# A decoder layer with routed experts: the low parts of w1 and w3 made once per expert and loaded from DRAM, in place of a subtraction per block

## The reference, cut to what matters

```python
x = layernorm(x + attn(x))                 # 8192 tokens of 128
x = layernorm(x + cross(x, ctx))
flat = x.reshape(-1, 128)
probs = softmax(flat @ gate_W.T); top_v, top_i = top_k(probs, 2)          # 8 experts, 2 per token
g = silu(einsum('td,edf->etf', flat, w1_e)); u = einsum('td,edf->etf', flat, w3_e)    # f = 512
routed = gates @ einsum('etf,efd->etd', g * u, w2_e)
shared = mean over 8 shared experts of (silu(x @ w1_s) * (x @ w3_s)) @ w2_s
out = layernorm(x + 0.5 * shared + 0.5 * routed)
```

## Time and profile before

| | |
|---|---|
| time, median of 3 runs | 739.44 us (737.78 to 742.28) |
| the profiled execution | 737.8 us |
| its span | 736.0 us |
| PE busy | 663.8 us, 90% |
| DVE, ACT, POOL busy | 511.9, 469.2 and 468.0 us |
| mean granted clock of TensorE | 0.964 of full |
| DMA | 72.70 MB, mean 99 GB/s |
| chain that ended last | PE 70%, DVE 13%, POOL 5%, ACT 5% of the span |

### The profile page before, as it was taken

One profiled execution on the slowest core, in us unless ns is written; L12 is line 12 of the kernel. 1 busy time (PEld: TensorE's weight loads), 2 busy tenths in 40 slices (PEclk: granted clock), 3 DMA queues, 4 the chain that ended last, 5 costly groups with the idle time before them and its releaser, 6 DMA issues.

```text
span 736.0 us, 16511 instructions
## 1 busy us (share of the span) xinstructions
PE 663.8 (90%) x5112; PEld 621.0 (84%) x5113; DVE 511.9 (70%) x1426; ACT 469.2 (64%) x1434; POOL 468.0 (64%) x471
## 2 busy tenths in 40 slices
PE   4899999978799999999999999999999999999700
PEld 3688888877588887899999999999999999998600
DVE  2689999986999973466556555565556555647995
ACT  4899999963389852365565455455555555646885
POOL 3488888886010147748888777777777777771332
PEclk9899999999989999999999999999999999999955
DMA  8467555553211216211111111121111212227683
GB/s 231 129 203 235 180 181 171 183 174 115 72 31 56 59 51 176 79 30 41 44 41 44 49 51 51 47 54 50 50 54 50 51 48 52 50 78 202 167 234 86
DMA packets 87250, 72.70 MB, mean 99 GB/s; under 512 B 10066, under 2 KB 72410, under 8 KB 87194
## 3 DMA queue, kind: packets, MB, share of 16 engines
q1 hardware_dynamic: 77808, 53.43, 24.7%
q0 software_dynamic: 9088, 18.63, 9.4%
q10 hardware_dynamic: 298, 0.01, 0.0%
HBM read 50.14 MB, written 21.89 MB: 98 GB/s over the span
## 4 chain that ended last, share of the span: by engine, by line
PE 70%; DVE 13%; POOL 5%; ACT 5%; issue 5%; DMA 1%; SPq 0%; POOLq 0%; DVEq 0%; ACTq 0%
PE bank L1516 16%; PE bank L1481 9%; PE bank L1483 9%; PE bank L1482 9%; PE bank L1142 5%; PE bank L547 4%; PE bank L1131 3%; PE bank L1132 3%; PE bank L1133 3%; POOL y_rows L1425 3%; PE bank L542 2%; DVE xg L1820 2%; PE bank L1473 2%; ACT ev L708 2%; PE bank L572 2%
## 5 line engine op out<-in xcount | busy, mean ns | idle before, releaser
L1611 DVE TENSOR_TENSOR s_hT<-s_sg,bank 128x512 f32<-128x512 f32 x142 | 97.7, 688 | 140.3 <-ACT s_sg L1552 80.9
L1425 POOL DMA_INDIRECT y_rows<-e_y,dst_tab x142 | 152.4, 1073 | 50.2 <-issue 42.0
L1417 POOL DMA_INDIRECT xg<-x_rows,src_tab x142 | 145.8, 1027 | 46.3 <-issue 39.6
L1481 PE MATMUL bank<-e_x_hi,e_w_hi 128*128 128x256 f32 x568 | 172.1, 303 | 0.0
L1483 PE MATMUL bank<-e_x_hi,e_w_lo 128*128 128x256 f32 x568 | 160.6, 283 | 0.0
L1482 PE MATMUL bank<-e_x_lo,e_w_hi 128*128 128x256 f32 x568 | 160.5, 283 | 0.0
L1516 PE MATMUL bank<-w,s_hT 128*128 x1136 | 138.2, 275 | 0.0
L1516 PEld LDWEIGHTS bank<-w,s_hT 128*128 128x128 f32 x1136 | 133.0, 192 | 0.0
L1558 ACT ACTIVATE e_y<-bank 128x256 f32<-128x256 f32 x71 | 27.2, 384 | 147.1 <-DMA y_rows<-e_y,dst_tab 111.7
L1482 PEld LDWEIGHTS bank<-e_x_lo,e_w_hi 128*128 128x128 f32 x568 | 109.1, 192 | 0.0
L1481 PEld LDWEIGHTS bank<-e_x_hi,e_w_hi 128*128 128x128 f32 x568 | 108.6, 191 | 0.0
(11 more groups left out here) (170 smaller groups left out, 1453.8 us busy)
## 6 DMA issues: line engine op xcount, KB each, us to landing
yk<-y_rows SPq DMA_DIRECT2D x16, 512.0 KB, 4.3
xT_in<-in_xT_dram SPq DMA_DIRECT2D x16, 256.0 KB, 3.0
x_res<-in_x_dram SPq DMA_DIRECT2D x16, 256.0 KB, 3.2
w_all<-in_L_ffn_w_e_dram SPq DMA_DIRECT2D x16, 256.0 KB, 4.0
c_in<-in_ctx_dram SPq DMA_DIRECT2D x16, 256.0 KB, 2.9
cT_in<-in_ctxT_dram SPq DMA_DIRECT2D x16, 256.0 KB, 3.1
x_rows<-x SPq DMA_DIRECT2D x16, 256.0 KB, 2.4
x2T_cols<-x2T SPq DMA_DIRECT2D x16, 256.0 KB, 2.8
```

The source lines that it names most:

```text
L1417: nc.gpsimd.indirect_dma_start(xg[b % XR][:, t, :], None, x2_rows, bass.IndirectOffsetOnAxis(src_tab[:, i:i + 1], 0)).then_inc(gathered[b ...
L1425: nc.gpsimd.indirect_dma_start(y_rows, bass.IndirectOffsetOnAxis(dst_tab[:, n:n + 1], 0), y[b % R][:, t, :], None).then_inc(scattered[b % ...
L1481: nc.tensor.matmul(at, w_hi[r % WR][:, w], x_hi[r % R][:, :], start=True, stop=False)
L1611: nc.vector.tensor_tensor(hT[par][:, half * HC:(half + 1) * HC, :].rearrange("p c n -> p (c n)"), sg[half][:, :], bank[2 + half][:, :], AL ...
```

## The change

The low part of w1 and w3 depends only on the expert. The change makes it once for each of the 8 experts, in the routing stage, and keeps the 8 in a DRAM tensor `w_lo_rows`, 512 KB each. ScalarE makes a high part into one of two tiles `split_hi`, GpSimd subtracts into one of two tiles `split_lo`, SP stores. In the experts stage SP loads the low part of each block by one DMA of 512 KB, and VectorE's `w_low` is gone. ScalarE still makes the high part for each block.

```diff
@@ attention, scalar, last
             if i == NG + 3:
                 take_x2T(*at(5))
+                act.wait_ge(all_ld, 16 * 3 * E)
+                split(0)
+                split(1)
                 early(0)
...
@@ routing, sync
+        def store_low(e):
+            sp.wait_ge(split_lo_ok, e + 1)
+            sp.dma_start(w_lo_rows[ds(e * P, P), :], split_lo[e % 2][:, :].bitcast(F32)).then_inc(split_stored[e % 2], 16)
         def rest():
             sp.wait_ge(attended.l_ps, NG)
             for g in range(EARLY):
                 if g + 3 < EARLY:
                     load_x(g + 3)
                 sp.dma_start(x2_all[:, ds(g * GT, GT), :], group_rows(x2_rows, g)).then_inc(all_ld[g // 2], 16)
+                if g < 2:
+                    for e in range(4 * g, 4 * g + 4):
+                        store_low(e)
@@ routing, gpsimd
+        def split(e):
+            pool.wait_ge(split_hi_ok, e + 1)
+            if e >= 2:
+                pool.wait_ge(split_stored[e % 2], 16 * (e // 2))
+            nc.gpsimd.tensor_tensor(split_lo[e % 2][:, :], columns_of(e), split_hi[e % 2][:, :].bitcast(F32),
+                                    ALU.subtract).then_inc(split_lo_ok, 1)
         def rest():
+            pool.wait_ge(attended.all_ld, 16 * 3 * E)
+            for e in range(4):
+                split(e)
             x_low(2)
+            for e in range(4, E):
+                split(e)
             x_low(3)
@@ routing, scalar
+        def split(e):
+            if e >= 2:
+                act.wait_ge(split_lo_ok, e - 1)
+            nc.scalar.activation(split_hi[e % 2][:, :], columns_of(e), ACT.Copy).then_inc(split_hi_ok, 1)
         def rest():
             for n in range(PRE, EARLY * FC):
                 chunk(n)
+                if 2 <= n - PRE + 2 < E:
+                    split(n - PRE + 2)
                 if 0 <= n - C0 < NC:
                     codes(n - C0)
@@ experts
+    def sync(sp):
+        at_reg = sp.alloc_register("e_lo_at")
+        sp.wait_ge(late.w_at_ok, 1)
+        for n in range(2):
+            sp.wait_ge(late.split_stored[n], 16 * (E // 2))
+        for b in range(NB):
+            sp.reg_load(at_reg, w_at[0:1, ds(b, 1)])
+            at = sp.snap(at_reg, min_val=0, max_val=(E - 1) * P)
+            if b >= WR:
+                sp.wait_ge(u_ps, (b - WR + 1) * 2)
+            sp.dma_start(w_lo[b % WR][:, :].bitcast(F32), w_lo_rows[ds(at, P), :]).then_inc(w_lo_ld[b % WR], 16)
...
-                pe.wait_ge(w_lo_ok, b + 1)
+                pe.wait_ge(w_lo_ld[r % WR], 16 * (j * (TURN // WR) + r // WR + 1))
...
-        def w_low(b):
-            dve.reg_load(at_reg, w_at[0:1, ds(b, 1)])
-            at = dve.snap(at_reg, min_val=0, max_val=(E - 1) * P)
-            if b >= WR:
-                dve.wait_ge(u_ps, (b - WR + 1) * 2)
-            dve.wait_ge(w_hi_ok, b + 1)
-            nc.vector.tensor_tensor(w_lo[b % WR][:, :], columns(w_all, at), w_hi[b % WR][:, :].bitcast(F32),
-                                    ALU.subtract).then_inc(w_lo_ok, 1)
```

More of the change, by code:

```diff
@@ L104, in __init__ @@
         self.w_at_ok = sem("w_at_ok")
+        self.split_hi = [one(f"split_hi{n}", [P, 2 * F], F32R) for n in range(2)]
+        self.split_lo = [one(f"split_lo{n}", [P, 2 * F], F32R) for n in range(2)]
+        self.split_hi_ok, self.split_lo_ok = sem("split_hi_ok"), sem("split_lo_ok")
+        self.split_stored = [sem(f"split_stored{n}") for n in range(2)]
 @dataclass
@@ L217, in _ @@
                     rest()
-                    two.sync(sp)
+                    late_x, out_rows_of = two.sync(sp)
+                    late_x()
+                    one.sync(sp)
+                    out_rows_of()
                 @block.gpsimd
@@ L239, in _ @@
                     ahead, run = one.scalar(act)
-                    early, rest = zero.scalar(act, ahead)
-                    first.scalar(act, early)
+                    early, split, rest = zero.scalar(act, ahead)
+                    first.scalar(act, early, split)
                     rest()
@@ L689, in tensor, with scalar @@
         pe.wait_ge(w2s_ld, 16)
-    def scalar(act, early):
+    def scalar(act, early, split):
         act.dma_start(bq_two[:, :].rearrange("a (j d) -> a j d", j=GT),
@@ L1219, in rest @@
                 ahead(n - EARLY * FC)
-        return chunk, rest
+        return chunk, split, rest
     def vector(dve, ahead):
@@ L1394, in experts @@
     w_hi = ring("w_hi", [P, 2 * F], F32R, n=WR)
+    y = ring("y", [P, BT, D])
     w_lo = ring("w_lo", [P, 2 * F], F32R, n=WR)
-    y = ring("y", [P, BT, D])
     sg, hT = late.sg, late.hT_of_block
-    w_hi_ok, w_lo_ok, xT_ps, x_hi_ok, x_lo_ok, g_ps, u_ps, sg_ok, h_ok, y_ps, y_ok = (
-        sem(f"e_{n}") for n in "w_hi_ok w_lo_ok xT_ps x_hi_ok x_lo_ok g_ps u_ps sg_ok h_ok y_ps y_ok".split())
+    w_hi_ok, xT_ps, x_hi_ok, x_lo_ok, g_ps, u_ps, sg_ok, h_ok, y_ps, y_ok = (
+        sem(f"e_{n}") for n in "w_hi_ok xT_ps x_hi_ok x_lo_ok g_ps u_ps sg_ok h_ok y_ps y_ok".split())
+    w_lo_ld = [sem(f"e_w_lo_ld{n}") for n in range(WR)]
     LATE_AT = (NB - 2, NB - 1)
@@ L1699, in store, with late_x, rest @@
             sp.dma_start(group_rows(out_rows, g), res[g % 2][:, :, :]).then_inc(stored[g % 2], 16)
-        LAG = R + 2
-        for i in range(4):
-            load_x(i)
-        for n in range(RING):
-            sp.wait_ge(scattered[n], 16 * BT * len(range(n, NB, RING)))
-        nx = 4
-        for g in range(NG + LAG):
-            if g < NG:
-                load(g)
-            while nx < LATE and FC * (nx - 1) + 1 < LEAD + 2 * (g - R + 2):
-                load_x(nx)
-                nx += 1
-            if g >= LAG:
-                store(g - LAG)
-        for n in range(2):
-            sp.wait_ge(stored[n], 16 * (NG // 2))
+        def late_x():
+            for i in range(2):
+                load_x(i)
+        def rest():
+            LAG = R + 2
+            for i in range(2, 4):
+                load_x(i)
+            for n in range(RING):
+                sp.wait_ge(scattered[n], 16 * BT * len(range(n, NB, RING)))
+            nx = 4
+            for g in range(NG + LAG):
+                if g < NG:
+                    load(g)
+                while nx < LATE and FC * (nx - 1) + 1 < LEAD + 2 * (g - R + 2):
+                    load_x(nx)
+                    nx += 1
+                if g >= LAG:
+                    store(g - LAG)
+            for n in range(2):
+                sp.wait_ge(stored[n], 16 * (NG // 2))
+        return late_x, rest
     def tensor(pe):
```

17 lines of the change are left out of this document (8 added, 9 removed).

## The result

| | before | after |
|---|---|---|
| time, median | 739.4 us (737.78 to 742.28) | 748.5 us (746.89 to 749.12) |
| ratio | | 1.0119, 95% interval 1.0098 to 1.0141 |
| the profiled execution | 737.8 us | 746.89 us |
| its span | 736.0 us | 745.2 us |
| DVE, ACT, POOL busy | 511.9, 469.2, 468.0 us | 438.7, 486.6, 468.5 us |

The change makes the kernel slower by 9.1 us, 1.2%. VectorE lost 73 us of work, and hardly any of that shows in the time.

A forecast was written before the change was run, and what follows sets the result against it. TensorE bounds the experts, and VectorE's chain to the first one-hots delays routing's table. Routing's +9.0 us less 0.7 us for shorter transfers gives +8.3 us: 739.4 + 8.3 = 747.7 us, range 740.5 to 753 (8 in 10).

The forecast's parts named there:

- What bounds the kernel: Experts: TensorE busy for all 346.04 us, 4.87 us a block; routing's table: three engines close to full, started by VectorE's chain.
- What is removed: Experts: 71 VectorE subtractions, 87.1 us, give nothing themselves; GpSimd's indirect transfers shorten, so the last scatter starts 0.7 us earlier.
- The experts' loads: Experts: 71 loads of 512 KB on SP, landing in 4.3 us with 14.6 us of lead, cost nothing.
- rival of late loads: Experts: low-part loads arrive late and TensorE waits at each block; 18 us more, 766 us; chance 0.07.
- first step: Routing, ScalarE: two high parts ahead of the last `x2T` delay it by 1.2 us; picks move from 184.9 to 186.0 us.
- Second step: Routing, GpSimd and stores: split 2 waits for store 0 until 191.5 us, then a nearly closed row of splits follows.
- Third step: Routing: VectorE's chain to the first one-hots waits for GpSimd's splits, 8.2 us in the first walk.
- collisions in the table's first rounds: Routing's table: further collisions of splits with one-hots were put at nothing, as TensorE is then the slower one.
- the signs: Expected in traces: TensorE's pre-table wait 10 us or more, first experts block at 319 to 321, `pos` operations 1.5 to 3 us.
- the splits hide: Routing rival: GpSimd's operations mostly miss VectorE's exposed ones; +1 to +4 us, 740.5 to 743.5 us; chance 0.24.
- ScalarE does wait for the splits: Routing rival: ScalarE's high parts wait for GpSimd and hold up the silus; +13 to +16 us, 752 to 756; chance 0.09.
- Nothing was faster: Experts rival: relieving GpSimd's backlog drops the pace below 4.87 us a block; 733 to 738 us with hidden splits; chance 0.04.

The follow-up runs named there:

- the experts' part alone: Against the changed kernel: no splits or stores in routing; each block's 512 KB load reads another tensor, same traffic, low parts wrong; 738.73 us, ratio 0.9993.
- the kernel with loads behind block b-2: Against the changed kernel: each low-part load in the experts is issued when block b-2's up products are done, not b-4's; 747.65 us, ratio 1.0109.
- the kernel with the small subtraction: Against the changed kernel: GpSimd's subtraction in routing covers 8 of 1024 columns; high parts, stores and waits stay; 742.09 us, ratio 1.0045.

## Why the prediction was right

**What bounds the kernel.** Right as put. The experts' stretch is 346.04 us in both kernels, and what VectorE loses there is not time. The kernel with the experts' part alone shows it by itself: within 1 us of before.

**What is removed.** The mechanism is as told: the transfers fell from 2.02 to 0.97 us, and the mean of 142 scatters to 975 ns, against 1063 where the subtraction stands in the experts. The size, 0.7 us, was too large for what reaches the end. The last scatter:

```profile
669.56 0.96 POOL L1482 DMA_INDIRECT y_rows<-e_y,dst_tab  x1 [0.30 <-issue]
```

It follows the experts' first matmul by 349.02 us; before it was 349.52. That is 0.5 us, of which 0.43 arrive at VectorE's first weighting of the combine stage. And most of that did not last: at VectorE's products in the combine stage there is a pause of 0.29 us that before has not, marked as issue, with no releaser in the trace. Behind it the lag behind before is 9.12 us, where it had been 8.77. Why it pauses there stays open; a third of a microsecond was not worth a run.

**The experts' loads: nothing.** Right. The landing time was taken as 4.3 us and is 3.7 where it can be read, in the kernel with loads behind block b-2. The lead was taken as 14.6 us and is 16.0. The DMA share rose from 0.18 to 0.50 of 4.87 us a block, so by an estimate from these a load takes 1.6 us of the DMA engines' time, not the 2.4 of my expectation above. The rival of late loads is out.

**Routing, first step.** Right to a tenth: the picks start at 186.55 us in place of 184.87, 1.68 us later, 0.59 of which are the drift of that execution. The rest, 1.09, was put at 1.2 (1.1 for the picks). The rows of ScalarE, beside the earlier trace rows:

```profile
176.60 0.60 ACT L772 ACTIVATE x2T<-bank 128x512 f32<-128x512 f32 x1 [1.91 <-PE bank L550]
177.09 2.00 ACT L1250 ACTIVATE split_hi<-w_all 128x1024 fp32r<-128x1024 f32 x2
...
183.21 0.60 ACT L772 ACTIVATE x2T<-bank 128x512 f32<-128x512 f32 x1 [0.56 <-PE bank L550]
```

**Second step.** The order of GpSimd's work was forecast as it fell: split 2 at 191.5 (191.83), `x_lo` at 196.5 (196.51), split 4 at 198.5 (198.21). From there the splits stood closer than I had them: split 6 ended at 205.73 and not at 207, since neither ScalarE's high parts nor the stores made GpSimd wait between them, as I had it in my walk.

**Third step.** The term was mis-sized in both of its parts, and the two errors nearly cancel. I had four waits, of 1.6, 2.4, 1.8 and 2.4 us, 8.2 together. There are four, and they measure 1.73 - 0.69 = 1.04, 2.66 - 0.69 = 1.97, 1.53 - 0.23 = 1.30 and 2.35 - 0.23 = 2.12 us (the short values from the kernel with the small subtraction, where the conversion and the shift each take 0.23 us): 6.4 us. The one-hots come clear of split 6. The first are done at 207.39 + 1.04 = 208.43 us, and not at 209.7.

Against that stands the sentence that collisions in the table's first rounds cost nothing, "as TensorE is then the slower one". That was wrong. Split 7 and the two operations behind it stretched a one-hot to 3.21 us and another to 1.88 us, and VectorE lost the little lead it had. Before, its row shows four waits in these rounds, of 0.68, 0.19, 0.19 and 0.22 us, three for TensorE and one for ScalarE, 1.28 together, and none behind the last of them until 259.60:

```profile
217.91 0.69 DVE L1340 TENSOR_TENSOR s_hT<-s_sg,bank 128x512 f32<-128x512 f32 x1 [0.22 <-PE bank L1133]
```

In the kernel after VectorE has no such wait from the first one-hots to 268.79 us. Its one-hots are lengthened by 3.5 us up to 230 us, against 1.1 before; 1.3 of these 2.4 us go into the waits that are gone, and 1.1 are left. From then on four rounds take VectorE 11.1 us, seen in the starts of GpSimd's `x_lo`, which wait for ScalarE and by it for VectorE's one-hots:

```profile
227.50 1.30 POOL L1121 TENSOR_TENSOR s_x_lo<-s_x2T,s_x_hi 128x512 fp32r<-128x512 f32 x1 [8.94 <-ACT s_x_hi L1223]
238.61 1.30 POOL L1121 TENSOR_TENSOR s_x_lo<-s_x2T,s_x_hi 128x512 fp32r<-128x512 f32 x1 [9.81 <-ACT s_x_hi L1223]
249.72 1.30 POOL L1121 TENSOR_TENSOR s_x_lo<-s_x2T,s_x_hi 128x512 fp32r<-128x512 f32 x1 [9.81 <-ACT s_x_hi L1223]
```

Four of TensorE's rounds at 2.71 us are 10.84 us. Before, these starts are 11.1 us apart too (218.33, 229.43, 240.52 us). So in the table's first rounds TensorE was the slower one before, as I had said, but by a hair, and from 218 us on VectorE is the slower one in both kernels. The lag at the first table matmul is 8.12 us (210.45 - 202.33), and at the experts' first matmul 9.19 us: 1.07 us that I had put at nothing.

**The sum**, from the two traces: 0.59 of drift, 1.09 for ScalarE, 6.43 for the four waits, 1.07 for the table's rounds, 0.43 given back by GpSimd, 0.35 lost at the pause in combine: 9.1 us, and the spans differ by 9.2. Predicted were 8.3. The forecast held because the largest term had the right mechanism, place and bounds (6.3 to 11), and, by luck, the misses of 1.8 us down and 1.1 us up stood against each other. Of the signs, TensorE's wait ahead of the table came out at 9.59 us, just under the 10 that I had named; the first block at 320.54 us, the products on `pos` and the blocks of 4.87 us are as told.

**The rivals.** That the splits hide is refuted by the four waits. ScalarE does wait for the splits, 2.27, 0.81 and 2.48 us, but VectorE's rows from 191 to 208 us show no wait for its silus. Nothing was faster: the experts' pace is still 4.87 us a block.

What a version without routing's cost could reach is known: it would be the experts' part alone, 738.73 us, which the measurement cannot tell from before.

## What to carry to other kernels

Ask of moved work which engine it will exclude, not only which engine has time: VectorE and GpSimd are two rows of the profile, yet with two inputs in SBUF on one and a reading operation on the other they run as one, and the pair's chain is what to walk. Take a chain that waits for nothing and lay the other engine's operations over it; the cost is the sum of what is left of each operation met, and an operation's length is only its upper bound. And a rate that two engines share within 3% (11.1 and 10.84 us here) has no slack on either, so a delay there is not hidden by calling one of them the slower.

## What the runs showed of the hardware

- A VectorE product with two fp32 inputs in SBUF, 0.69 us alone, took 1.73 and 2.66 us beside GpSimd subtractions that read SBUF, and 0.69 us beside GpSimd fills that only write.
- Small conversions and shifts of 128x128 on VectorE, 0.23 us alone, took 1.53 and 2.35 us beside the subtractions, and up to 0.42 us beside the fills.
- It works both ways. Six indirect transfers of GpSimd, 0.94 us alone, took 4.65 us more in all beside VectorE subtractions of 128x1024 in fp32. The rule of the Trainium skill ("SBUF — State Buffer", section "Who interferes with whom") that such a subtraction does not stall the writing of descriptors is not borne out by these rows.
- The subtraction of 128x1024 on GpSimd took 2.36 us (two in 4.72), 2.8 where it met VectorE's work; on VectorE 1.22 us.
- After waits of 4.57 us before and 9.59 us after, TensorE ran at a granted clock of 0.50 for about 5 us in both kernels, and at 1.00 or near it behind that.
- Loads of 512 KB from DRAM, one each 4.87 us at a DMA share of 0.50, landed in 3.7 us with no effect on TensorE when issued 6.2 us ahead of use; issued 1.4 us ahead (landing in 3.6 us, at a DMA share of 0.33) they made it wait 2.1 to 2.2 us a block.
